# First linear of each GNN layer in groups of 512 nodes instead of 256, with the products chunk by chunk and the next group's turns between the chunks

## Chip, cores and metric

The kernel runs on one core of a Trainium2 chip. The metric is the device time of one execution in microseconds (us). One program computes a whole network; the change touches one of its stages, which runs four times.

## The reference, cut to what matters

The network works on 10000 nodes of 512 features. It has a relational graph layer, a mixture of experts, four graph layers of the kind below, and a quantized feed-forward part. The change touches `((1 + eps) * x + agg) @ W1 + b1` and what feeds its batch statistics:

```python
def _gine_layer(x, src, dst, edge_attr, eps, We, be, W1, b1, gamma, beta, W2, b2):
    e = edge_attr @ We + be
    m = jax.nn.relu(x[src] + e)
    agg = jax.ops.segment_sum(m, dst, num_segments=x.shape[0])
    h = ((1.0 + eps) * x + agg) @ W1 + b1        # the stage that changes
    mu = jnp.mean(h, axis=0)
    var = jnp.mean(jnp.square(h - mu), axis=0)
    h = (h - mu) * jax.lax.rsqrt(var + BN_EPS) * gamma + beta
    h = jax.nn.relu(h)
    return jax.nn.relu(h @ W2 + b2)
...
x = x + _L1_gnn_ref(_layernorm(x, axis=-1), ...)   # four such layers; the first reads layer-normed rows
```

## The kernel before, in words

Each of the four layers has three stages, kept apart by barriers on all engines: `message_phase` (gather, messages, sums per node), `hidden_phase` (the first linear, L2065 to L2215) and an output stage (the second linear). The layers are called first (layer 0), inner (layers 1 and 2, one loop body run twice) and final (layer 3); tiles carry these words in their names.

`hidden_phase` takes the nodes in `NG` = 40 groups: 39 of `GROUP` = 256 nodes and a last one of 16. A group goes through these steps, each on its own engine and each written as a loop over the groups by `static_pipeline`, which fixes the order of the work on every engine in advance:

- SP loads the 256 rows of x into `xin` (two buffers, which are halves of the weight buffer `raw`); a load waits until the turns of the group two before are done. The first 512 rows were loaded by the message stage. At the end SP fetches the next weight into `raw`.
- GpSimd gathers the aggregated sums, 128 rows at a time, into a ring of three buffers `agg` (L2109); gather j waits for mix j - 2. In layer 0 it also computes the row's reciprocal deviation `rs` (L183).
- In layer 0 alone (`normal`), VectorE takes the row statistics (L164, L168, L175), then `nb` (L2185), and ScalarE normalizes the rows in place (L2158).
- VectorE mixes: `(1 + eps) * x + agg` (L2196), one instruction for 128 rows.
- TensorE turns the mixed rows, eight 128x128 transposes a group into the PSUM tile `T` (L2132).
- ScalarE copies `T` to `xh` (L1177, the high part), VectorE subtracts to get `xl` (L1183, the low part), each one instruction over 4 chunks of 256 columns.
- TensorE forms the products (L783 to L785, called `three`): for each of 4 output chunks, for each of 4 input chunks, three matmuls with 256 moving columns: 48 a group. `xh`, `xl`, `T` and the result tile `O` have two buffers each; the two `T` take four PSUM banks and the two `O` the other four.
- ScalarE adds the bias and stores the four result chunks to `hT` (L2153), and VectorE takes batch statistics of pairs of groups (L2208).

TensorE's order is: turns of group g + 1, then products of group g. `keep_awake` (L791) runs matmuls on an identity at the start of a stage.

Of the kernel before, what the change touches and what calls it, by code (L numbers as in the profile page):

```python
# [10 lines left out]
P = 128  # L11
# [20 lines left out]
PAIRS = NG // 2 + 1  # L32
# [2032 lines left out]
def hidden_phase(core, cst, ed, table, eps, b1, w, layer, hT, stats, normal):  # L2065
# [5 lines left out]
    R, W = 3, 2  # L2071
    tiles = [(g, t, n) for g in range(NG) for t, n in tiles_of(g == NG - 1)]
    names = "eps eps1 b1 ld0 ld1 mix T hi lo M ev bn stats aggr var rstd nb nx w2 swg0 swg1 swg2"
    with core.phase("hidden", names) as (s, sbuf, psum):
        e_t = sbuf("eps", [P, 1])
        b1t = sbuf("b1", [P, KC])
        xin = [raw[:, q * TILES:(q + 1) * TILES, :] for q in range(2)]
        rbn, mv = ([sbuf(f"{n}{q}", [P, TILES, k]) for q in range(W)] for n, k in (("rbn", 6), ("mv", 2)))
        rs, nb = ([sbuf(f"{n}{q}", [P, TILES]) for q in range(W)] for n in ("rs", "nb"))
        agg = [sbuf(f"agg{i}", [P, D]) for i in range(R)]  # L2080
        xh = [sbuf(f"xh{q}", [P, KC, GROUP], F32R) for q in range(2)]
        xl = [sbuf(f"xl{q}", [P, KC, GROUP], F32R) for q in range(2)]
# [3 lines left out]
        last = lambda g: g == NG - 1  # L2086
        at = lambda g: slice(g * GROUP, g * GROUP + width_of(last(g)))
        mixed = lambda g: min((g + 1) * TILES, len(tiles))
        with nc.Block() as block:
            @block.sync  # L2090
            def _(eng):
# [7 lines left out]
                eng.wait_ge(s["T"], NG)  # L2099
# [4 lines left out]
            def _(eng):  # L2104
                def gather(j):
                    g, t, n = tiles[j]
                    c = g * TILES + t
# [3 lines left out]
                def rstd(g):  # L2111
                    wait(eng, s["nx"], g - W + 1)
                    row_rstd(eng, s, g, mv[g % W], cst.half, rs[g % W], last(g))

                if normal:
                    for j in range(R - TILES):
                        gather(j)
                    for g in range(NG):
                        for j in range(g * TILES + R - TILES, min(len(tiles), (g + 1) * TILES + R - TILES)):
                            gather(j)  # L2120
                        rstd(g)
                else:
                    static_pipeline([(0, gather)], len(tiles))
# [25 lines left out]
            def _(eng):  # L2149
# [12 lines left out]
                def high(g):  # L2162
                    split_hi(eng, s, g, g % 2, last(g), T, xh)
# [724 lines left out]
```

## Time and profile before

| | us |
|---|---|
| three runs | 4548.05, 4555.41, 4559.69 |
| median | 4555.41 |
| profiled execution, its own time | 4532.05 |
| its span in the trace | 4530.3 |
| mean granted clock of TensorE in the span | 0.913 |

Busy shares of the span: TensorE matmul 90%, its weight loads 74%, VectorE 61%, ScalarE 46%, GpSimd 34%. These are averages over stages with different limits. A matmul's duration in the trace is longer than its distance to the next one, since matmuls are pipelined: the distance from start to start is what a matmul costs in a dense row of them. The same holds, to a smaller degree, for dense rows of instructions on ScalarE and VectorE.

### The profile page before, as it was taken

The numbers are of one execution on the slowest core, as the hardware profiler recorded it, in microseconds if no ns is written. First come the engines' busy times: TensorE is split into PE (matmuls) and PEld (weight loads), VectorE is DVE, ScalarE is ACT, GpSimd is POOL, SyncE is SP. The second block draws the span as 40 slices with busy tenths as digits, with TensorE's granted clock in tenths as the row PEclk, the third lists the DMA queues.
The fourth block names the chain that finished last, engine by engine and source line by source line (L and its number), as shares of the span: only waits on it lengthen the run. The fifth ranks groups of instructions, "written<-read, shape, count | busy, mean of one in ns | idle before, by whom it ended". The sixth has DMA issues, their size and how long they took to land. (4 is left out here: it accounts for less than half of the span.)

```text
span 4530.3 us, 64838 instructions
## 1 busy us (share of the span) xinstructions
PE 4092.3 (90%) x22630; PEld 3331.6 (74%) x22630; DVE 2776.7 (61%) x5314; ACT 2065.9 (46%) x3536; POOL 1541.3 (34%) x1482
## 2 busy tenths in 40 slices
PE   7887899899978868789999999999899998999977
PEld 3446788777767656549988579987599784998855
DVE  5665656578975567557854455543555444556878
ACT  1222223333348334365567543475433674334556
POOL 1442266217840658744410233201332004330033
PEclk9998999999999568789999999999899998999965
DMA  8995478539975869874422565323754237554678
GB/s 302 400 336 179 151 261 283 183 123 348 390 273 163 296 143 174 156 234 153 155 89 106 172 205 165 107 94 136 237 162 140 77 119 242 159 161 126 185 194 248
DMA packets 460259, 886.19 MB, mean 196 GB/s; under 512 B 70660, under 2 KB 111221, under 8 KB 459182
## 3 DMA queue, kind: packets, MB, share of 16 engines
q1 hardware_dynamic: 291386, 520.05, 33.8%
q0 software_dynamic: 90016, 237.51, 18.9%
q10 hardware_dynamic: 78568, 124.88, 7.9%
q8 instruction: 168, 2.75, 0.2%
q14 instruction: 121, 0.99, 0.1%
HBM read 609.61 MB, written 303.62 MB: 202 GB/s over the span
## 5 line engine op out<-in xcount | busy, mean ns | idle before, releaser
L2109 POOL DMA_INDIRECT hidden_agg<-edge_sums,edge_where x316 | 354.6, 1122 | 711.3 <-DVE layer_raw_inner L2196 284.3
L1942 POOL DMA_INDIRECT message_x<-g,edge_partner x120 | 115.8, 965 | 755.6 <-POOLq L150 458.3
L783 PE MATMUL hidden_O<-hidden_xh,layer_hi_inner 128*128 128x256 f32 (+1 forms) x1280 | 366.9, 287 | 0.1
L785 PE MATMUL hidden_O<-hidden_xl,layer_hi_inner 128*128 128x256 f32 (+1 forms) x1280 | 361.0, 282 | 0.0
L784 PE MATMUL hidden_O<-hidden_xh,layer_lo_inner 128*128 128x256 f32 (+1 forms) x1280 | 360.2, 281 | 0.0
L2153 ACT ACTIVATE hT_inner<-hidden_O,hidden_b 128x256 f32<-128x256 f32 (+1 forms) x320 | 124.1, 471 | 332.6 <-PE hidden_O L785 332.6
L783 PE MATMUL root_O<-root_hi,root_xh 128*128 128x512 f32 (+1 forms) x632 | 255.4, 404 | 11.4 <-DVE root_xl L1183 10.2
L783 PE MATMUL output_O<-layer_hi_inner,output_hh 128*128 128x512 f32 (+1 forms) x632 | 250.2, 396 | 1.8 <-DVE output_hl L2290 1.8
L785 PE MATMUL output_O<-layer_lo_inner,output_hh 128*128 128x512 f32 (+1 forms) x632 | 249.7, 395 | 0.0
L784 PE MATMUL output_O<-layer_hi_inner,output_hl 128*128 128x512 f32 (+1 forms) x632 | 249.6, 395 | 0.0
L785 PE MATMUL root_O<-root_lo,root_xh 128*128 128x512 f32 (+1 forms) x632 | 247.9, 392 | 0.0
L2299 DVE TENSOR_TENSOR layer_raw_inner<-output_O,output_b2t 128x1024 f32<-128x1024 f32 x80 | 96.9, 1211 | 246.3 <-PE output_O L785 246.3
L784 PE MATMUL root_O<-root_hi,root_xl 128*128 128x512 f32 (+1 forms) x632 | 247.6, 392 | 0.0
L784 PEld LDWEIGHTS hidden_O<-hidden_xh,layer_lo_inner 128*128 128x128 f32 x1280 | 243.3, 190 | 0.0
L783 PEld LDWEIGHTS hidden_O<-hidden_xh,layer_hi_inner 128*128 128x128 f32 x1280 | 242.8, 190 | 0.6 <-DVE hidden_xl L1183 0.6
L785 PEld LDWEIGHTS hidden_O<-hidden_xl,layer_hi_inner 128*128 128x128 f32 x1280 | 243.0, 190 | 0.0
L1071 POOL DMA_INDIRECT root_agg<-edge_sums,edge_where x158 | 179.4, 1136 | 151.1 <-POOLq L150 68.7
L2208 DVE BATCH_NORM_STATS2 h_stats<-hT_inner 128x6 f32<-128x512 f32 (+2 forms) x168 | 97.6, 644 | 170.9 <-ACT hT_inner L2153 170.9
L1183 DVE TENSOR_TENSOR hidden_xl<-hidden_T,hidden_xh 128x1024 fp32r<-128x1024 f32 (+1 forms) x160 | 190.8, 1192 | 13.1 <-ACT hidden_xh L1177 13.1
L1078 POOL DMA_INDIRECT root_add<-edge_sums,edge_where_next x158 | 176.5, 1117 | 52.6 <-issue 47.3
L1177 ACT ACTIVATE hidden_xh<-hidden_T 128x1024 fp32r<-128x1024 f32 (+1 forms) x160 | 163.4, 1021 | 63.1 <-PE hidden_T L2132 61.4
L1177 ACT ACTIVATE root_xh<-root_T 128x1024 fp32r<-128x1024 f32 x80 | 80.5, 1008 | 243.9 <-PE root_O L785 87.9
(503 smaller groups left out, 12712.9 us busy)
## 6 DMA issues: line engine op xcount, KB each, us to landing
edge_sums<-message_res SPq DMA_DIRECT2D x160, 256.0 KB, 2.1
layer_raw_inner<-g SPq DMA_DIRECT2D x78, 512.0 KB
g<-layer_raw_inner SPq DMA_DIRECT2D x78, 512.0 KB
room<-in_L_gnn_basis SPq DMA_DIRECT2D x30, 1280.0 KB
order_basis<-in_L_gnn_basis SPq DMA_DIRECT2D x18, 1280.0 KB
edge_sums<-relation_res SPq DMA_DIRECT2D x82, 256.0 KB
order_x<-in_x SPq DMA_DIRECT2D x39, 512.0 KB
normed<-order_y ACTq DMA_DIRECT2D x39, 512.0 KB
```

The source lines that it names most:

```text
L783: eng.matmul(out, a_hi, b_hi, start=start, stop=False)
L784: eng.matmul(out, a_lo, b_hi, start=False, stop=False)
L785: return eng.matmul(out, a_hi, b_lo, start=False, stop=stop)
L1071: eng.indirect_dma_start(agg[q][0:n, t, :], None, ed.sums[0], bass.IndirectOffsetOnAxis(ap=ed.where[0][0:n, j:j + 1], axis=0)).then_inc(ga ...
L1078: eng.indirect_dma_start(add[q][0:n, t, :], None, ed.sums[0], bass.IndirectOffsetOnAxis(ap=ed.where_next[0:n, j:j + 1], axis=0), bounds_ch ...
L1177: eng.activation(xh[q][:, :, 0:w], T[q][:, :, 0:w], ACT.Copy).then_inc(s["hi"], 1)
L1183: eng.tensor_tensor(xl[q][:, :, 0:w], T[q][:, :, 0:w], xh[q][:, :, 0:w].bitcast(F32), ALU.subtract).then_inc(s["lo"], 1)
L1942: eng.indirect_dma_start(x[t % R][:, :], None, table, bass.IndirectOffsetOnAxis(ap=ed.partner[1][:, t:t + 1], axis=0)).then_inc(ga[t % R], 16)
L2109: eng.indirect_dma_start(agg[j % R][0:n, :], None, ed.sums[1], bass.IndirectOffsetOnAxis(ap=ed.where[1][0:n, c:c + 1], axis=0)).then_inc(g ...
L2153: m = eng.activation(hT[:, o, at(g)], O[g % 2][:, o, 0:width_of(last(g))], ACT.Identity, bias=b1t[:, o:o + 1])
L2208: eng.bn_stats(stats[:, o, g // 2 + last(g), :], hT[:, o, (g if g in alone else g - 1) * GROUP:at(g).stop]).then_inc(s["bn"], 1)
L2299: eng.tensor_tensor(part(y[q], last), part(O[q], last), b2t[0:n, :].unsqueeze(1).to_broadcast([n, k, D]), ALU.add).then_inc(s["add"], 1)
```

## The change

A group has `WIDE_GROUP` = 512 nodes (`PAIRS` = 20 groups: 19 of 512 and one of 272). `xin` becomes all of `raw` for even groups, and for odd groups the columns of `hT` that belong to the last but one group. Loads are of 512 rows. `T` is four whole PSUM banks, one for each input chunk, and `O` four, one for each output chunk; `xh` and `xl` have one buffer each, split by chunk. ScalarE's copy, VectorE's subtraction, and ScalarE's result step now work on one chunk of 512 columns each. TensorE does the products of input chunk c for all four output chunks (12 matmuls of 512 columns), then the four turns of chunk c of the next group, then chunk c + 1. The order on ScalarE and VectorE is written out by hand. The ring of gathers keeps its three buffers.

```diff
-    R, W = 3, 2
+    R = 3
+    PT = WIDE_GROUP // P
...
-        xin = [raw[:, q * TILES:(q + 1) * TILES, :] for q in range(2)]
+        xin = [raw.ap(), hT[:, :, at(PAIRS - 2)]]
-        xh = [sbuf(f"xh{q}", [P, KC, GROUP], F32R) for q in range(2)]
-        T = [psum(f"T{q}", [P, KC, GROUP]) for q in range(2)]
-        O = [psum(f"O{q}", [P, KC, GROUP]) for q in range(2)]
+        xh = sbuf("xh", [P, KC, WIDE_GROUP], F32R)
+        T = [psum(f"T{c}", [P, WIDE_GROUP]) for c in range(KC)]
+        O = [psum(f"O{o}", [P, WIDE_GROUP]) for o in range(KC)]
...
 SP
-                for g in range(2, NG):
-                    eng.wait_ge(s["T"], g - 1)
-                    eng.dma_start(part(xin[g % 2], last(g)), rows(table, g, last(g))).then_inc(ld[g % 2], 16)
+                for p in range(1, PAIRS):
+                    wait(eng, s["T"], (p - 1) * KC)
+                    f, begin = full(p), p * WIDE_GROUP
+                    eng.dma_start(xin[p % 2][:, 0:f, :], table[begin:begin + f * P, :]...).then_inc(ld[p % 2], 16)
...
 GpSimd
+                for j in range(R):
+                    gather(j)
+                for p in range(PAIRS):
+                    if normal:
+                        rstd(p)
+                    for j in range(p * PT + R, min(len(tiles), (p + 1) * PT + R)):
+                        gather(j)
...
 TensorE
-                static_pipeline([(0, turn_rows), (1, product)], NG)
+                turn_first()
+                for p in range(PAIRS):
+                    for c in range(KC):
+                        product(p, c)
+                        if p + 2 < PAIRS:
+                            turn_chunk(p + 1, c)
+                        elif p + 1 < PAIRS and c == 0:
+                            for each in range(KC):
+                                turn_chunk(p + 1, each)
...
 ScalarE
-                if normal:
-                    static_pipeline([(1, high), (0, norm), (2, evacuate)], NG)
+                for p in range(PAIRS):
+                    if p + 1 < PAIRS:
+                        high(p + 1, 0)
+                        high(p + 1, 1)
+                    if normal and p + 2 < PAIRS:
+                        norm(p + 2)
+                    if p + 1 < PAIRS:
+                        high(p + 1, 2)
+                    for o in range(KC):
+                        evacuate(p, o)
+                    if p + 1 < PAIRS:
+                        high(p + 1, 3)
...
 VectorE
-                if normal:
-                    static_pipeline([(4, statistics(0, KC - 1)), (1, shift), (2, low), (4, statistics(KC - 1, KC)), (1, mix), (0, row_statistics)], NG)
+                if normal:
+                    rows_ready(0)
+                for t in range(PT):
+                    mix(0, t)
+                for c in range(KC):
+                    low(0, c)
+                if normal:
+                    rows_ready(1)
+                for t in range(PT):
+                    mix(1, t)
+                for p in range(PAIRS):
+                    more, far = p + 1 < PAIRS, p + 2 < PAIRS
+                    if p >= 1:
+                        statistics(p - 1)
+                    if normal and far:
+                        row_statistics(p + 2)
+                    if more:
+                        low(p + 1, 0)
+                    if normal and far:
+                        shift(p + 2)
+                    if far:
+                        mix(p + 2, 0)
+                    if more:
+                        low(p + 1, 1)
+                    if far:
+                        mix(p + 2, 1)
+                    if more:
+                        low(p + 1, 2)
+                    if far:
+                        mix(p + 2, 2)
+                        mix(p + 2, 3)
+                    if more:
+                        low(p + 1, 3)
+                statistics(PAIRS - 1)
```

The waits that go with it: `turn_chunk(p, 0)` waits for all four mixes of group p; `product(p, c)` waits for `low(p, c)` and, at c = 0, for `evacuate(p - 1, o)` before output chunk o; `evacuate(p, o)` waits for the last matmul of output chunk o; `high` and `low` wait for the turns and the copy of their chunk. For the last group, `high` also waits until the products of the group before are nearly done, since `xh` has one buffer.

## Rows read from the trace of the kernel before

**Rows 1.** The page's first line.

```profile
span 4530.3 us, 64838 instructions
```

**Rows 2.** Windows by stage: hidden of layer 0, output of layer 0, hidden of layer 1; PE, PEld, DVE, ACT, POOL busy us (instructions), clock, DMA.

```profile
2050.00:2322.00 272.00, 269.53 (x2224) 265.59 (x2222) 207.80 (x418) 153.54 (x273) 108.18 (x111) 0.98 0.46 145
2330.00:2560.00 230.00, 225.09 (x966) 179.28 (x965) 96.07 (x85) 160.65 (x241) 2.14 (x3) 0.99 0.28 102
...
2657.00:2921.00 264.00, 262.66 (x2221) 262.33 (x2220) 143.38 (x199) 97.02 (x199) 82.50 (x73) 0.99 0.47 150
```

**Rows 3.** Timeline of TensorE, steady stretch of layer 1's hidden stage.

```profile
2800.81 1.04 PE L2132 MATMUL hidden_T<-cst_ident,layer_raw_inner 128*128 128x128 f32 x8
2801.61 0.36 PE L783 MATMUL hidden_O<-hidden_xh,layer_hi_inner 128*128 128x256 f32 x1
2801.81 0.28 PE L784 MATMUL hidden_O<-hidden_xh,layer_lo_inner 128*128 128x256 f32 x1
...
2899.31 1.04 PE L2132 MATMUL hidden_T<-cst_ident,layer_raw_inner 128*128 128x128 f32 x8
```

**Rows 4.** Timeline of TensorE: products 512 columns wide, in two other stages.

```profile
704.73 1.03 PE L1048 MATMUL root_T<-cst_ident,root_xin 128*128 128x128 f32 x8
...
705.84 0.39 PE L784 MATMUL root_O<-root_hi,root_xl 128*128 128x512 f32 x1
...
711.08 1.04 PE L1048 MATMUL root_T<-cst_ident,root_xin 128*128 128x128 f32 x8
...
2449.78 0.40 PE L785 MATMUL output_O<-layer_lo_first,output_hh 128*128 128x512 f32 x1
...
2455.85 0.40 PE L784 MATMUL output_O<-layer_hi_first,output_hl 128*128 128x512 f32 x1
```

**Rows 5.** Timeline of the 16-column group, layer 1, and a window over it.

```profile
2912.11 0.17 PE L783 MATMUL hidden_O<-hidden_xh,layer_hi_inner 128*128 128x16 f32 x1
...
2919.34 0.36 PE L785 MATMUL hidden_O<-hidden_xl,layer_hi_inner 128*128 128x16 f32 x1
...
2910.50:2920.00 9.50, 9.20 (x63) 9.10 (x62) 1.83 (x6) 0.74 0.05 20
```

**Rows 6.** Timelines of the beginnings: layer 1 (three rows), layer 0 (two rows).

```profile
2651.58 0.96 POOL L2109 DMA_INDIRECT hidden_agg<-edge_sums,edge_where  x1 [1.10 <-DVE layer_raw_inner L2196]
2655.17 0.75 DVE L2196 SCALAR_TENSOR_TENSOR layer_raw_inner<-layer_raw_inner,hidden_eps,hidden_agg 128x512 f32<-128x512 f32 x1 [0.96 <-DMA hidden_agg<-edge_sums,edge_where]
2657.11 0.39 PE L783 MATMUL hidden_O<-hidden_xh,layer_hi_inner 128*128 128x256 f32 x1
...
2036.79 1.29 DVE L164 BATCH_NORM_STATS2 hidden_rbn<-layer_raw_first 128x6 f32<-128x512 f32 x2
2050.40 0.56 PE L783 MATMUL hidden_O<-hidden_xh,layer_hi_first 128*128 128x256 f32 x1
```

**Rows 7.** Timelines and one group of lines: what ScalarE, VectorE and GpSimd instructions take.

```profile
2125.97 1.29 DVE L164 BATCH_NORM_STATS2 hidden_rbn<-layer_raw_first 128x6 f32<-128x512 f32 x2 [0.34 <-DMA layer_raw_first<-x]
2127.07 1.04 ACT L1177 ACTIVATE hidden_xh<-hidden_T 128x1024 fp32r<-128x1024 f32 x1
2127.95 0.72 POOL L183 TENSOR_TENSOR hidden_rs<-hidden_mv,cst_half 128x2 f32<-128x2 f32 x1
2128.86 1.22 DVE L1183 TENSOR_TENSOR hidden_xl<-hidden_T,hidden_xh 128x1024 fp32r<-128x1024 f32 x1
2128.98 1.52 ACT L2158 ACTIVATE layer_raw_first<-layer_raw_first,hidden_nb,hidden_rs 128x512 f32<-128x512 f32 x2 [0.87 <-DVE hidden_nb L2185]
...
2152.64 1.57 ACT L2153 ACTIVATE hT_first<-hidden_O,hidden_b 128x256 f32<-128x256 f32 x4 [1.47 <-PE hidden_O L785]
...
2789.49 2.47 DVE L2208 BATCH_NORM_STATS2 h_stats<-hT_inner 128x6 f32<-128x512 f32 x4 [4.17 <-ACT hT_inner L2153]
...
2924.94 1.41 POOL L2261 TENSOR_TENSOR output_rs<-output_mv,cst_half 128x4 f32<-128x4 f32 x1 [34.60 <-DVE output_mv L2269]
...
L2012 ACT ACTIVATE message_res<-message_B 128x512 f32<-128x512 f32 x5 | 2.8, 600 | 0.1
```

More of the change, by code:

```diff
@@ L2110, in gather, with rstd @@
                                            bass.IndirectOffsetOnAxis(ap=ed.where[1][0:n, c:c + 1], axis=0)).then_inc(ga[j % R], 16)
-                def rstd(g):
-                    wait(eng, s["nx"], g - W + 1)
-                    row_rstd(eng, s, g, mv[g % W], cst.half, rs[g % W], last(g))
-                if normal:
-                    for j in range(R - TILES):
-                        gather(j)
[L2118 to L2123, printed above, removed]
+                def rstd(p):
+                    wait(eng, s["nx"], through(p - 2) if p >= 2 else 0)
+                    eng.wait_ge(s["var"], p + 1)
+                    for n, ts in spans(p):
+                        m = eng.tensor_tensor(rs[p % 2][0:n, ts], mv[p % 2][0:n, ts, 1], cst.half[0:n, 0:ts.stop - ts.start], ALU.pow)
+                    m.then_inc(s["rstd"], 1)
@@ L2162, in high, with evacuate, norm @@
-                def high(g):
-                    split_hi(eng, s, g, g % 2, last(g), T, xh)
+                def evacuate(p, o):
+                    eng.wait_ge(s["M"], p * KC + o + 1)
+                    eng.activation(hT[:, o, at(p)], O[o][:, 0:width(p)], ACT.Identity, bias=b1t[:, o:o + 1]).then_inc(s["ev"], 1)
+                def norm(p):
+                    eng.wait_ge(s["nb"], p + 1)
+                    for t, n in tiles_of_pair(p):
+                        m = eng.activation(xin[p % 2][0:n, t, :], xin[p % 2][0:n, t, :], ACT.Identity,
+                                           bias=nb[p % 2][0:n, t:t + 1], scale=rs[p % 2][0:n, t:t + 1])
+                        m.then_inc(s["nx"], 1)
@@ L2164, in _, with high @@
+                def high(p, c):
+                    eng.wait_ge(s["T"], p * KC + c + 1)
+                    if p == PAIRS - 1:
+                        eng.wait_ge(s["M"], p * KC if c == KC - 1 else (p - 1) * KC + 1)
+                    eng.activation(xh[:, c, 0:width(p)], T[c][:, 0:width(p)], ACT.Copy).then_inc(s["hi"], 1)
                 eng.wait_ge(s["b1"], 16)
                 if normal:
-                    static_pipeline([(1, high), (0, norm), (2, evacuate)], NG)
-                else:
-                    static_pipeline([(0, high), (1, evacuate)], NG)
+                    norm(0)
@@ L2199, in statistics @@
-                def statistics(first, end):
-                    alone = range(NG - 2, NG)
-                    def step(g):
-                        if g % 2 == 0 and g not in alone:
-                            return
-                        eng.wait_ge(s["ev"], g + 1)
-                        for o in range(first, end):
-                            eng.bn_stats(stats[:, o, g // 2 + last(g), :], hT[:, o, (g if g in alone else g - 1) * GROUP:at(g).stop]).then_inc(s["bn"], 1)
-                    return step
@@ new lines, in statistics, with low, rows_ready @@
+                def statistics(p):
+                    for o in range(KC):
+                        eng.wait_ge(s["ev"], p * KC + o + 1)
+                        eng.bn_stats(stats[:, o, p, :], hT[:, o, at(p)]).then_inc(s["bn"], 1)
+                def low(p, c):
+                    eng.wait_ge(s["hi"], p * KC + c + 1)
+                    eng.tensor_tensor(xl[:, c, 0:width(p)], T[c][:, 0:width(p)], xh[:, c, 0:width(p)].bitcast(F32), ALU.subtract).then_inc(s["lo"], 1)
+                def rows_ready(p):
+                    row_statistics(p)
+                    shift(p)
```

138 lines of the change are left out of this document (78 added, 60 removed).

## Prediction

> **What bounds the kernel now.** I read the windows by stage first [rows 2]. The four hidden stages take 272 us in layer 0 and about 264 us in each of layers 1 to 3 (one of the three is shown; the others are alike), of a span of 4530.3 us [rows 1]. In all four TensorE is busy for 99% of the window at a granted clock of 0.98 or 0.99, so its own work sets the time. In layers 1 to 3 VectorE is busy 54% and ScalarE 37%, but in layer 0 VectorE is busy 207.8 of 272 us: the other engines have room in three layers and little in one. The timeline of TensorE then gives its prices, as distances from start to start.
>
> A steady group of 256 nodes takes (2899.31 - 2800.81) / 15 = 6.57 us [rows 3]: eight turns 0.80 us, one matmul 0.08 us late behind them, and 48 matmuls at 0.1185 us. Thus 512 nodes cost 13.13 us. The group of 16 nodes is nearly as dear as a full one: its 48 matmuls run from 2912.11 to 2919.34, 7.4 us, and the granted clock of that window falls to 0.74 on average, a mix of 2.4 and 1.2 GHz [rows 5].
>
> **TensorE's own work.** A matmul of 512 columns costs (711.08 - 705.84) / 23 = 0.228 us in the root stage, where 23 of them stand between those rows, and (2455.85 - 2449.78) / 26 = 0.2335 us in the output stage [rows 4]. I take 0.2305 between them, as nothing says which of the two this stage will resemble. One matmul of 512 then replaces two of 256 (0.237). The turns stay at 0.10 us each, but there are four switches in 512 nodes instead of two, each followed by a matmul that is 0.09 us late (704.73 to 705.84 is 1.11: 0.80 of turns, 0.23, and 0.09) [rows 4]. A group of 512: 48 x 0.2305 + 16 x 0.10 + 4 x 0.09 = 13.02 us, against 13.13: 0.1 us less, times 19 = 2 us a layer. With 0.228 and 0.2335 it is 4 us less or 1 us more. The width itself brings almost nothing, because a row of 256 is already paced near its columns.
>
> The last group: 256 columns at 0.1185 us and 16 more in proportion are about 0.126 us each, 6.05 us, where before there were 5.7 + 7.4 plus a small turn. This takes 7.3 us off each layer and is the one sure gain. At the end `high` of the last group waits for the group before, and the four result steps of 0.6 us come slower than the three matmuls of 0.38 us that wait for each: 1 us back.
>
> **The beginning of layers 1 to 3.** Before, the first product starts at 2657.11, 1.2 us after the fourth mix (2655.17 + 0.75) [rows 6], since the turns of group 1 come ahead of it. Now it also waits for four mixes, then a turn, a copy of 0.6 us (the 512-wide copy of L2012) [rows 7] and a subtraction of 0.67 us (half of 1.22 and a little): about 2657.8. Then comes a new wait. `turn_chunk(1, 0)` stands behind the first 12 matmuls (2.8 us, till 2660.5) and needs all four mixes of the second group. VectorE gets to them only after the four subtractions, at 2659.5. The gather of the fourth waits for the first of these mixes, since the ring has three buffers, and a gather takes 2655.17 - 2651.58 = 3.6 us to be usable [rows 6]. So 2660.2 + 0.3 + 3.6 = 2664.1, mix done at 2664.8. TensorE stands for 4.3 us, with product(0, 1) and everything else queued behind. Before, layer 0's first matmul took 0.56 us instead of 0.36 [rows 6, 3]: the lower level of the clock, 1.2 GHz. Its window lost 0.02 x 272 = 5.4 us to that level [rows 2], of which the last group's window has 0.26 x 9.5 = 2.5 [rows 5]; a cold start thus costs up to 3 us, and I add 2. Against the start of before this is 0.7 + 4.3 + 2 = 7 us.
>
> Sum for such a layer: -7.3 - 2 + 1 + 7 = about -1.5 to -2, say -2; three layers -6 us. Bounds: -8 (no low clock, 0.228) to +4 (0.2335, loads of 1 MB delaying the gathers at the start).
>
> **The steady state of layers 1 to 3.** VectorE has for 512 nodes four statistics (2.47 us for four), four subtractions (2.7) and four mixes (3.0): 8.2 of 13.0 us; ScalarE four copies (2.4) and four result steps (2.4). The load of 1 MB starts at T(p, 3) and has 6 us until the first mix wants it, 15 until TensorE does. These stay hidden; if the load took over 15 us it would not.
>
> **Layer 0.** Here the hand-written orders make a ring. `low(p, 3)` must be done before VectorE takes `statistics(p-1)` and `row_statistics(p+2)`; GpSimd's `rs` and VectorE's `nb` follow; `norm(p+2)` stands on ScalarE ahead of `high(p+1, 2)`, the four `evacuate(p, o)` and `high(p+1, 3)`; and `low(p+1, 3)` waits for that. Its length [rows 7]:
>
> - low: 0.06 + 0.67 us.
> - Batch statistics, four in a row: 2.4.
> - From the first row statistic to the first normalized row: before, 2128.98 - 2125.97 = 3.01 for two tiles. Two tiles more: 2 x 0.61 for the statistics, 0.17 for the aggregates, and `rs` on four columns takes 1.41 instead of 0.72: 5.1.
> - norm, four tiles: 1.52 + 2 x 0.71 = 2.9.
> - high: a copy of 512 takes 0.60, 0.53 in a row.
> - evacuate: 256 columns are 0.37 apart (1.57 for four); 256 columns more are (1.04 - 0.60) / 2 = 0.22: 4 x 0.59 = 2.4.
> - high again: 0.53.
>
> Together 14.6 us, against TensorE's 13.0: here the ring sets the time, and TensorE idles 1.6 us a group, in front of product(p+1, 0), which waits for evacuate(p, 0). Overlaps that I price too low or high give 13.8 to 15.2.
>
> ScalarE's result step is the row's extrapolation. The Trainium skill (ScalarE: Activation LUTs, section "What ACT_TABLE_LOAD costs") has 280 ns + 0.833 ns a column with a bias operand and 93 ns of overlap: 0.61 us at 512, an estimate, which would make the ring 0.1 us longer.
>
> The beginning: row statistics start at 2036.79 [rows 6], norm 5.1 later, first mix at 2042.7; the fourth waits for its gather until 2047.3 (2043.4 + 0.3 + 3.6); first product about 2049.7, against 2050.40. Then `rows_ready(1)` comes behind four subtractions (2051.5), its norm at 2056.6, mix(1, 0) done 2058.2, the gather for mix(1, 3) at 2062.1, done 2062.8. TensorE idles 10 us and starts again at the lower clock (2 us). Three more chunks of 3.26 us, and `high(1, 3)` ends at about 2076. Then 17 turns of the ring: 2076 + 17 x 14.6 = 2324.2. product(18, 0) starts 2.3 us before that; 12.4 for it, 0.7 and 6.05 for the last group: 2341. Before, the last product ends at about 2321.5. Layer 0 thus loses 20 us (6 at a ring of 13.8, 30 at 15.2).
>
> **Sum.** -6 + 20 = +14 us, on the profiled 4532 us: 4546. The three runs shown have the median 4555.4, 23 us above the profiled one, with no stage to put it to; I forecast against the median: 4569 us. Differences of 0.3% (13.7 us) are about what a measurement of this kernel tells from no change.
>
> **Rivals.**
>
> 1. *The ring does not bind (faster, or no change).* If its pieces overlap more and it falls to TensorE's 13.0 us, layer 0 gets 17 x 1.6 = 27 us back: -13, 4542. For it: TensorE was the limit in layer 0 too, at 207.8 us of VectorE work, and that work stays. Against it: the length is a sum of waits in a fixed order, not of busy time. The sign turns at a ring of 13.8 us. With the gathers at the start also in time (-4.3 -2 us in three layers) it is 4524. Chance 0.20.
> 2. *The gather of the fourth tile enters the ring.* gather(p+2, 3) waits for mix(p+2, 0) and has 4.5 us until `low(p+1, 3)` is due; it took 3.6 us with loads of 512 KB in flight. If the 1 MB load, which starts in the same microseconds, makes it 5 us or more, each group of layer 0 gains 0.7 to 1.5: +12 to +25 on the sum, 4581 to 4594. Chance 0.17.
> 3. *The clock falls at TensorE's idle of each group.* Before, layer 0 starts on the low level behind its long waits [rows 6], and the steady stretch has nearly none of it. If 1.6 us were enough, each group of layer 0 would lose up to 2 us of products, of which the idle absorbs most; +10 or so: 4580. Chance 0.08.
> 4. *Four banks in turn.* The output stage runs 512-wide products at clock 0.99 [rows 2], but twelve at a time into one bank; now the bank changes after every three. If the clock fell once in each wide group for the 2 us above, 57 groups in three layers would lose 114 us, and layer 0's 19, partly inside their idle, some 10: 4693. The Trainium skill (TensorE: Matmul & The Clock Gate, section "A second HAM failure mode: psum-queue depth-cycling") tells of 512-column products that cycle through banks, idle a little between groups and make the clock swing. No row of before cycles whole banks so. Chance 0.03.
>
> My forecast keeps 0.52. Its range is 4549 to 4587 (ring 13.8 to 15.2, the layers' bounds). The range that holds the time 8 times in 10 takes in rival 2 and the upper part of rival 1: 4532 to 4596. Faster by over 0.3%: the deeper half of rival 1 and a little of a common gain from 0.228, 0.18. Within 0.3%: a third of the forecast's case and the rest of rival 1, 0.39. Slower: 0.43.
>
> **What would show it.** In the changed profile: layers 1 to 3 hidden stages of 260 to 264 us from first to last product, TensorE idle once for about 4 us behind the first 12 matmuls, `hidden_T` waiting for the mix; matmuls of 512 at 0.23 us; no 16-column matmuls. In layer 0: about 290 us, TensorE waiting for `hT_first` (L783 behind the result step) 1 to 2 us a group, ScalarE's norm waiting for `nb`, and a distance of 14.6 us from group to group. The forecast is wrong if layer 0's groups are 13 us apart, or if those of the other layers are not.

## The result and the profile after

The changed kernel is slower by 0.8%: median 4585.89 us over 5 runs (4579.85 to 4587.9), against 4548.05 us over 5 runs (4538.01 to 4559.69) of the kernel before beside it. The ratio is 1.0077, 95% interval 1.0061 to 1.0094: +28 to +43 us against the kernel before beside it, where the forecast was +14. The page's first line of after, for the profiled execution ([rows 1] for before):

```profile
span 4584.1 us, 56575 instructions
```

Windows over the four hidden stages after, from first to last product (columns as in [rows 2]; layer 0, then layers 1 to 3):

```profile
2048.00:2361.00 313.00, 275.67 (x1258) 221.13 (x1259) 205.84 (x422) 141.17 (x231) 89.86 (x92) 0.92 0.38 123
2699.00:2962.00 263.00, 258.07 (x1256) 209.85 (x1257) 149.60 (x231) 96.24 (x157) 72.60 (x74) 0.98 0.47 148
3307.00:3568.00 261.00, 252.01 (x1248) 205.42 (x1248) 146.65 (x229) 95.70 (x156) 69.72 (x72) 0.99 0.47 146
3904.50:4165.00 260.50, 257.33 (x1260) 209.49 (x1260) 147.95 (x231) 95.91 (x157) 70.76 (x72) 0.98 0.47 148
```

Layer 0 took 272 us from first to last product at clock 0.98; now it takes 313 at 0.92, and TensorE is idle for 37 us of them. The other three are about as long as before. A fairer measure takes the start of a stage in: from the first `keep_awake` matmul of the hidden stage to the first one of the output stage. I use it below for every kernel.

| us per stage | layer 0 | layer 1 | layer 2 | layer 3 |
|---|---|---|---|---|
| before | 289.9 | 275.8 | 275.9 | 277.6 |
| after | 330.9 | 278.7 | 279.8 | 277.3 |

Layer 0: +41.0. Layers 1 to 3: +2.9, +3.9, -0.3. Their sum, 47.5 us, is nearly all of the 53.8 by which the profiled spans differ. The medians differ by 38; the profiled execution of before was faster than its median.

**The pace of layer 0.** Timeline of ScalarE, layer 0 after: the normalizations of three groups in a row (L2190; a group's four instructions are one row), and what stands behind the late one.

```profile
2196.50 2.94 ACT L2190 ACTIVATE layer_raw_first<-layer_raw_first,hidden_nb,hidden_rs 128x512 f32<-128x512 f32 x4 [2.27 <-DVE hidden_nb L2244]
...
2213.91 2.93 ACT L2190 ACTIVATE hT_first<-hT_first,hidden_nb,hidden_rs 128x512 f32<-128x512 f32 x4 [5.93 <-DVE hidden_nb L2244]
2216.75 0.58 ACT L2198 ACTIVATE hidden_xh<-hidden_T 128x512 fp32r<-128x512 f32 x1
2217.23 2.40 ACT L2185 ACTIVATE hT_first<-hidden_O,hidden_b 128x512 f32<-128x512 f32 x4
...
2228.11 2.94 ACT L2190 ACTIVATE layer_raw_first<-layer_raw_first,hidden_nb,hidden_rs 128x512 f32<-128x512 f32 x4
```

The distances are 17.4 and 14.2 us: the group in the buffer `hT` is late, the next one, in `raw`, less so. Over groups 2 to 18 the mean is 16.0 us, where I forecast 14.6. The timelines of SP, VectorE and TensorE show why the late one is late, and under them two rows of the waits of that stage (us in total, times, longest):

```profile
2200.10 0.36 SPq L2107 DMA_DIRECT2D hT_first<-x  x1
...
2209.32 2.47 DVE L2229 BATCH_NORM_STATS2 hidden_rbn<-hT_first 128x6 f32<-128x512 f32 x4 [3.51 <-DMA hT_first<-x]
...
2233.36 0.60 PE L2141 MATMUL hidden_T<-cst_ident,hT_first 128*128 128x128 f32 x4
2233.99 0.36 SPq L2107 DMA_DIRECT2D hT_first<-x  x1
```

```profile
PE hidden_O L784 <- DVE hidden_xl L2266: 30.2, 12, 4.2
DVE hidden_rbn L2229 <- DMA hT_first<-x: 23.1, 8, 4.0
```

The 1 MB load issued at 2200.10 released the row statistics at 2209.32, 9.2 us later. For layers 1 to 3 I had written that it "has 6 us until the first mix wants it". In layer 0 the first to want it is not the mix but VectorE's row statistics, which stand at the front of the ring. Statistics, norm and mixes of these rows follow, then their turns between the chunks of products, the last at 2233.36, and only then is the buffer free for its next load (2233.99): 33.9 us for two groups.

There is a second, smaller wait. Before every other group VectorE stands at the fourth mix of the group ahead until its gather has landed, though the copy that its next subtraction needs is done. The 1 MB load of the other buffer (issued at 2182.28 here) is in flight beside this gather, which makes it the likely cause. Timelines of ScalarE and VectorE:

```profile
2186.78 0.60 ACT L2198 ACTIVATE hidden_xh<-hidden_T 128x512 fp32r<-128x512 f32 x1
2188.28 0.75 DVE L2256 SCALAR_TENSOR_TENSOR hT_first<-hT_first,hidden_eps,hidden_agg 128x512 f32<-128x512 f32 x1 [2.29 <-DMA hidden_agg<-edge_sums,edge_where]
2188.95 0.69 DVE L2266 TENSOR_TENSOR hidden_xl<-hidden_T,hidden_xh 128x512 fp32r<-128x512 f32 x1
```

Eight subtractions are late by 0.5 to 2.7 us in this way, 10 us in the stage. Together with the 23.1 us of waits for loads this is nearly all by which 17 groups exceed the pace of 13.8 us that the kernel with three loads shows below.

TensorE's own timeline at that place, and windows of 4 us over it:

```profile
2213.23 0.60 PE L2141 MATMUL hidden_T<-cst_ident,layer_raw_first 128*128 128x128 f32 x4
2218.05 0.76 PE L784 MATMUL hidden_O<-hidden_xh,layer_hi_first 128*128 128x512 f32 x1 [4.21 <-DVE hidden_xl L2266]
2218.61 0.63 PE L785 MATMUL hidden_O<-hidden_xh,layer_lo_first 128*128 128x512 f32 x1
2219.03 0.63 PE L786 MATMUL hidden_O<-hidden_xl,layer_hi_first 128*128 128x512 f32 x1
```

```profile
2208.00:2212.00 4.00, 4.00 (x21) 3.27 (x20) 2.64 (x7) 0.00 (x0) 0.00 (x0) 1.00 0.07 26
2216.00:2220.00 4.00, 1.96 (x5) 1.60 (x6) 2.22 (x5) 4.00 (x8) 2.73 (x3) 0.65 0.86 323
2220.00:2224.00 4.00, 4.00 (x13) 3.12 (x12) 4.00 (x7) 0.11 (x1) 0.96 (x1) 0.50 0.50 156
2224.00:2228.00 4.00, 4.00 (x21) 3.31 (x20) 3.23 (x11) 1.08 (x2) 1.03 (x1) 1.00 0.01 3
```

TensorE stands for 4.21 us. The row names `hidden_xl`, but that had been done: product(p+1, 0) waits for evacuate(p, 0), which ScalarE starts at 2217.23 behind the late norm. After this idle time the matmuls are 0.42 us apart instead of 0.23: the granted clock is 0.50, the level of 1.2 GHz, from about 2217.2 until about 2224.0. Something like it happens at every other group between 2086 and 2316: eight idle stretches of 1.9 to 4.2 us, some 32 us apart, and at each of them a fall to 0.50 for some microseconds. At the other groups TensorE idles at most 0.8 us and the clock stays at 1.00.

**The beginning of layer 1 after**, timelines of VectorE and TensorE ([rows 6] for before):

```profile
2692.03 0.75 DVE L2256 SCALAR_TENSOR_TENSOR layer_raw_inner<-layer_raw_inner,hidden_eps,hidden_agg 128x512 f32<-128x512 f32 x1 [2.60 <-DMA hidden_agg<-edge_sums,edge_where]
2695.86 2.14 DVE L2256 SCALAR_TENSOR_TENSOR layer_raw_inner<-layer_raw_inner,hidden_eps,hidden_agg 128x512 f32<-128x512 f32 x3 [3.08 <-DMA hidden_agg<-edge_sums,edge_where]
...
2709.42 1.11 PE L2141 MATMUL hidden_T<-cst_ident,hT_inner 128*128 128x128 f32 x4 [4.08 <-DVE hT_inner L2256]
...
2715.03 0.63 PE L786 MATMUL hidden_O<-hidden_xl,layer_hi_inner 128*128 128x512 f32 x1
```

```profile
2702.00:2705.00 3.00, 3.00 (x8) 2.03 (x7) 0.25 (x1) 0.00 (x0) 0.94 (x1) 0.50 0.98 352
2705.50:2708.50 3.00, 0.00 (x0) 0.00 (x0) 1.11 (x2) 0.00 (x0) 0.95 (x1) 1.00 0.32 100
2709.00:2715.40 6.40, 5.98 (x16) 4.77 (x17) 1.72 (x3) 0.60 (x1) 3.08 (x3) 0.50 0.43 127
```

The stall of 4.08 us ahead of the turns of group 1 is where the prediction put it; in layers 2 and 3 it is 6.6 and 3.1 us. But the first product comes 13.3 us after the stage's first matmul (2686.58 to 2699.86), before 10.7 (2646.42 to 2657.11); in layers 2 and 3 it is 2.7 and 3.5 us later than before. In layer 1 the first 24 matmuls run at the low level, until about 2715.5. These are two falls and not one: the windows, whose third number from the end is the granted clock, show 0.50 in the first 12 matmuls, 1.00 during the stall, and 0.50 again behind it. In layer 2 the first 12 matmuls run at the high level and only those behind the stall at the low one.

In layer 0 the first product is 15.3 us behind the stage's first matmul (before 16.3), the stall ahead of group 1's turns is 7.3 us, and the granted clock is 0.50 for 15 of the first 19 us of products, before for the first 4.5.

### The profile page after: what moved, and what is told of

It reads as the page before. It is cut to its first block and busy times, and to the rows that moved or that the text cites. A ratio compares the mean times of both kernels' runs of the same rounds, so it can differ in the third digit from the quotient of the medians.

```text
span 4584.1 us, 56575 instructions
## 1 busy us (share of the span) xinstructions
PE 4078.2 (89%) x18790; PEld 3117.7 (68%) x18790; DVE 2789.4 (61%) x5420; ACT 2055.5 (45%) x3376; POOL 1488.7 (32%) x1463
## 5 line engine op out<-in xcount | busy, mean ns | idle before, releaser
L2198 ACT ACTIVATE hidden_xh<-hidden_T 128x512 fp32r<-128x512 f32 (+1 forms) x320 | 185.5, 587 | 655.4 <-PE hidden_T L2141 598.5
L2266 DVE TENSOR_TENSOR hidden_xl<-hidden_T,hidden_xh 128x512 fp32r<-128x512 f32 (+1 forms) x320 | 214.6, 676 | 175.9 <-ACT hidden_xh L2198 169.9
L784 PE MATMUL hidden_O<-hidden_xh,layer_hi_inner 128*128 128x512 f32 (+1 forms) x640 | 264.8, 414 | 2.2 <-DVE hidden_xl L2266 2.2
L786 PE MATMUL hidden_O<-hidden_xl,layer_hi_inner 128*128 128x512 f32 (+1 forms) x640 | 251.7, 393 | 0.0
L785 PE MATMUL hidden_O<-hidden_xh,layer_lo_inner 128*128 128x512 f32 (+1 forms) x640 | 250.5, 391 | 0.0
L657 PE MATMUL order_cb_ps<-room,order_spread 128*128 128x512 f32 x300 | 143.1, 623 | 28.7 <-DMA room<-in_L_gnn_basis 20.4
L784 PE MATMUL hidden_O<-hidden_xh,layer_hi_first 128*128 128x512 f32 (+1 forms) x320 | 139.0, 434 | 30.3 <-DVE hidden_xl L2266 30.2
L2406 ACT ACTIVATE hT_inner<-hT_inner,output_shf,output_scl (+2 forms) x312 | 159.6, 583 | 0.0
L1340 POOL TENSOR_TENSOR tokens_y<-tokens_y,tokens_rsd 128x1024 f32<-128x1024 f32 (+1 forms) x40 | 96.0, 2400 | 190.7 <-ACT tokens_y L1449 190.7
L1132 DVE TENSOR_TENSOR root_y<-root_O,root_agg 128x1024 f32<-128x1024 f32 x80 | 96.5, 1207 | 97.1 <-PE root_O L786 86.1
```

The lines of the kernel that those rows point to most:

```text
L657: m = eng.matmul(cb_ps[j % 2][:, :], spread[n][:, k, :], ba_t[i % RING][:, k % UNIT, :], start=k == 0, stop=k == SHARE - 1)
L784: eng.matmul(out, a_hi, b_hi, start=start, stop=False)
L785: eng.matmul(out, a_lo, b_hi, start=False, stop=False)
L786: return eng.matmul(out, a_hi, b_lo, start=False, stop=stop)
L2198: eng.activation(xh[:, c, 0:width(p)], T[c][:, 0:width(p)], ACT.Copy).then_inc(s["hi"], 1)
L2266: eng.tensor_tensor(xl[:, c, 0:width(p)], T[c][:, 0:width(p)], xh[:, c, 0:width(p)].bitcast(F32), ALU.subtract).then_inc(s["lo"], 1)
```

## Experiments

Ratios are to the kernel before, measured beside each on the same chip, with 95% intervals; the fourth column is the difference of the medians. Stage times are those of the one profiled execution. The chips differ: beside the last three kernels of the table the kernel before has a median of 4495.5 us, beside the others 4545 to 4548. The part of the profiled span outside the four stages, which no edit is meant to change, also differs from execution to execution: 3405 to 3447 us in the first nine kernels. So a stage's time is read for what an edit does in it, and the ratio for what it is worth.

| kernel | ratio | interval | us | layer 0 | layers 1, 2, 3 |
|---|---|---|---|---|---|
| changed | 1.0077 | 1.0061 to 1.0094 | +37.8 | 330.9 | 278.7, 279.8, 277.3 |
| layer 0 narrow | 1.0016 | 0.9996 to 1.0035 | +7.4 | 288.1 | 276.9, 278.2, 278.2 |
| layer 0 wide alone | 1.0094 | 1.0068 to 1.0119 | +39.9 | 316.0 | 275.3, 277.3, 277.4 |
| three loads | 1.0068 | 1.0043 to 1.0093 | +27.5 | 300.3 | 279.1, 279.7, 277.7 |
| statistics later | 1.0092 | 1.0069 to 1.0115 | +37.9 | 321.8 | 279.3, 278.3, 276.8 |
| both of these | 1.0002 | 0.9982 to 1.0023 | +5.0 | 284.6 | 279.1, 278.9, 277.4 |
| other beginning | 1.0015 | 0.9993 to 1.0038 | +10.4 | 329.3 | 268.0, 270.6, 267.7 |
| all three | 0.9956 | 0.9936 to 0.9976 | -18.6 | 280.7 | 271.6, 269.9, 269.0 |
| narrow, other beginning | 0.9951 | 0.9929 to 0.9974 | -23.6 | 288.5 | 267.6, 268.7, 268.2 |
| order alone | 1.0063 | 1.0039 to 1.0087 | +30.8 | 316.9 | 271.2, 271.6, 271.3 |
| load later alone | 1.0074 | 1.0044 to 1.0105 | +38.7 | 330.9 | 275.1, 275.8, 275.4 |
| three loads in layer 0 only | 0.9941 | 0.9921 to 0.9961 | -24.1 | 281.2 | 268.0, 268.6, 268.7 |

### Which layers

The narrow form of before (256 nodes, its batch statistics of the last two groups merged into one) in layer 0, and the reverse:

```diff
-                hidden_phase(core, cst, ed, table,
+                (narrow_hidden_phase if first else hidden_phase)(core, cst, ed, table,
```

> Layer 0's stage as before the change (groups of 256), layers 1 to 3 as after it. If the loss sits in layer 0, as the stage times say (+41 us there, about 0 in layers 1 to 3), this runs within 5 us of the kernel before, about 38 us under the changed kernel. If instead the wide form costs a little in every layer and layer 0's reading is an accident of one execution, it stays some 25 us or more over the kernel before.

> The reverse: the wide form in layer 0 alone, layers 1 to 3 as before the change. Loss in layer 0: about 38 us over the kernel before, within 5 us of the changed kernel. Loss spread over the layers: about 10 us over the kernel before.

+7.4 and +39.9 us: most of the loss is layer 0's. The first interval (-2 to +16 us) leaves room for the 1 to 3 us a layer that the stage times show for layers 1 to 3, and at its lower edge for no loss there at all.

The second kernel's trace also showed something new: its layer 0 has the same code as the changed kernel's and took 316.0 us, not 330.9. Its first half alternates like the one above; its second half does not. VectorE's timeline there:

```profile
2196.51 2.47 DVE L2229 BATCH_NORM_STATS2 hidden_rbn<-layer_raw_first 128x6 f32<-128x512 f32 x4 [0.50 <-DMA layer_raw_first<-x]
2210.32 2.46 DVE L2229 BATCH_NORM_STATS2 hidden_rbn<-hT_first 128x6 f32<-128x512 f32 x4
2224.91 2.48 DVE L2229 BATCH_NORM_STATS2 hidden_rbn<-layer_raw_first 128x6 f32<-128x512 f32 x4 [0.60 <-DMA layer_raw_first<-x]
```

Groups come evenly, 14.4 us apart (from 2186.63 to 2287.70 in seven), and a load issued at 2218.46 lands within 6.5 us. So the stage has two patterns, an even one near my 14.6 and an alternating one of 16, and slips from one to the other. Two kernels below give the same reading: "load later alone" has the changed kernel's layer 0 and took 330.9 us; "other beginning" and "order alone" have one and the same layer 0 and took 329.3 and 316.9. What makes it slip I did not find.

### The load or the ring

```diff
-        xin = [raw.ap(), hT[:, :, at(PAIRS - 2)]]
+        xin = [raw.ap(), hT[:, :, at(PAIRS - 2)], hT[:, :, at(PAIRS - 3)]]
-                    wait(eng, s["T"], (p - 1) * KC)
+                    wait(eng, s["T"], (p - 2) * KC)
```

> A third buffer for the table's rows, so that the 1 MB load of a group is issued one group (13 to 16 us) earlier. Theory A: in layer 0 every other group is held by a late load (row statistics wait 3.5 to 4.2 us on it, 23.1 us in 8 waits), and TensorE's idle behind it (about 4 us) is what lowers the clock; with the load early the waits on it fall to about 0, a group of layer 0 takes what the ring of VectorE, GpSimd and ScalarE takes, 14.2 to 14.8 us instead of a mean of 16.0, the granted clock stays at 1.0, and the time is 25 to 30 us under the changed kernel. Theory B: the four whole banks, or the clock by itself, make layer 0 slow: the group stays near 16 us and the time within 5 us of the changed kernel. Theory C: the ring alone makes 16 us and the wait on the load only takes up its slack: no wait on loads, still 15.5 to 16 us a group, less than 8 us gained.

The row statistics no longer wait for loads, the alternation is gone, and steady groups are 13.79 us apart (a few are longer, the mean over groups 2 to 18 is 14.05; timeline of ScalarE, then a window over eight groups):

```profile
2185.76 2.94 ACT L2190 ACTIVATE hT_first<-hT_first,hidden_nb,hidden_rs 128x512 f32<-128x512 f32 x4 [2.88 <-DVE hidden_nb L2244]
2199.54 2.94 ACT L2190 ACTIVATE hT_first<-hT_first,hidden_nb,hidden_rs 128x512 f32<-128x512 f32 x4 [2.30 <-DVE hidden_nb L2244]
2213.33 2.94 ACT L2190 ACTIVATE layer_raw_first<-layer_raw_first,hidden_nb,hidden_rs 128x512 f32<-128x512 f32 x4 [2.31 <-DVE hidden_nb L2244]
2227.12 2.94 ACT L2190 ACTIVATE hT_first<-hT_first,hidden_nb,hidden_rs 128x512 f32<-128x512 f32 x4 [2.31 <-DVE hidden_nb L2244]
```

```profile
2145.00:2255.00 110.00, 104.66 (x510) 84.09 (x509) 86.40 (x176) 58.27 (x96) 39.24 (x40) 1.00 0.46 153
```

TensorE still idles a little in each group (12.0 us in 16 waits, the longest 1.2), and behind those the clock stays at 1.00. Theory A's mechanism holds by the trace: no wait for a load, no fall of the clock, 30.6 us off layer 0's stage; its pace of 14.2 to 14.8 us a group was too long. By the medians only 10 to 12 us were gained instead of 25 to 30, and the interval overlaps that of the changed kernel. This kernel's six runs scatter from 4558 to 4592 us, and the profiled execution is the fastest of them; in time the gain of this edit by itself is not shown.

```diff
                 def statistics(p, first=0, end=KC):
...
-                    if p >= 1:
-                        statistics(p - 1)
                     if normal and far:
                         row_statistics(p + 2)
...
                         mix(p + 2, 1)
+                    if p >= 1:
+                        statistics(p - 1, 0, 2)
...
                         mix(p + 2, 2)
+                    if p >= 1:
+                        statistics(p - 1, 2, KC)
```

> VectorE's four statistics of the group behind are moved from ahead of the row statistics to behind the mixes 1 and 2 of the group ahead, in all layers; loads as after the change. If the ring (low of the last chunk, statistics, row statistics, GpSimd, shift, norm, high, evacuations) is what sets the groups whose load is in time, these get about 2 us shorter (from some 15 us to 13), and the groups with a late load stay near 17 or gain less, since the load is issued off TensorE's last turn and takes 8 us whatever VectorE does: 8 to 15 us under the changed kernel. If the load alone set the pace of both kinds of group, no change within 4 us.

No gain in the median, where 8 to 15 us were expected; the profiled layer 0 is 321.8 us, inside what the same form showed without this edit (316.0 and 330.9). Group by group the expectation is met in the middle of the stage: between groups 6 and 16 the late groups come 17.1 to 17.4 us behind the one before, the others 12.9 to 13.8. VectorE gets to its row statistics 2.4 us earlier and waits there: 39.6 us in 9 waits for the load, instead of 23.1 in 8. So with two buffers the load binds first and the ring behind it.

> The third buffer of the run with three loads and the statistics of the group behind moved back, together. With three loads a group of layer 0 took a regular 13.8 us, and nothing waited for a load. If that is the ring of VectorE, GpSimd and ScalarE, in which the four statistics take 2.4 us, moving them takes the ring under TensorE's own 13.0 us a group: layer 0's groups come at 13.0 us, the stage is some 15 us shorter than with three loads alone (285 instead of 300 us from its first TensorE instruction to the output stage's), and the time 12 to 18 us under that run, within 15 us of the kernel before. If 13.8 us is TensorE's own (turns, first products behind them), nothing changes against three loads alone, within 4 us.

The two together are worth more than their sum: the ratio falls to 1.0002, with an interval clear of the changed kernel's. ScalarE's timeline and a window of that kernel:

```profile
2195.96 2.92 ACT L2190 ACTIVATE hT_first<-hT_first,hidden_nb,hidden_rs 128x512 f32<-128x512 f32 x4
2208.92 2.93 ACT L2190 ACTIVATE layer_raw_first<-layer_raw_first,hidden_nb,hidden_rs 128x512 f32<-128x512 f32 x4
2221.88 2.92 ACT L2190 ACTIVATE hT_first<-hT_first,hidden_nb,hidden_rs 128x512 f32<-128x512 f32 x4
```

```profile
2145.00:2255.00 110.00, 110.00 (x545) 89.64 (x545) 91.03 (x187) 67.69 (x105) 42.18 (x43) 1.00 0.48 158
```

12.96 us a group, TensorE busy all the time, the stage 284.6 us (expected 285) and 15.7 shorter than with three loads alone. Behind the first groups the norm no longer waits for `nb`. That the ring of VectorE, GpSimd and ScalarE made 13.79 us is thereby shown: 2.4 us less in it, and TensorE sets the pace again.

### The beginning of a stage

```diff
+                for c in range(KC):
+                    product(0, c)
+                    for each in ((), (), (0, 1, 2), (3,))[c]:
+                        turn_chunk(1, each)
-                for p in range(PAIRS):
+                for p in range(1, PAIRS):
...
 SP, ahead of the load of group p
+                    if p == 1 and not normal:
+                        eng.wait_ge(s["mix"], 3)
```

> The changed kernel with another beginning of each stage only: TensorE does the products of chunks 0 to 2 of group 0 before the first turns of group 1, and in layers 1 to 3 the 1 MB load of group 1 waits for the third mix. Theory: the beginning of layers 1 to 3 costs about 10 us each (first product 2.6 us later because the load slows the gathers, 4.1 us stall ahead of the turns of group 1, half clock until some 13 us later). Then each of these stages gets 5 to 7 us shorter, layer 0 0 to 5 us (its pace is set by the loads), and the time is 15 to 25 us under the changed kernel. Rival: the wide groups of the steady state lose what is lost and the start does not matter: under 6 us gained.

Layers 1 to 3 are 10.7, 9.2 and 9.6 us shorter than after the change, more than expected; layer 0, paced by its loads, 1.6. The medians say 27 us less, where 15 to 25 were expected (the two kernels were measured on different chips, each beside the kernel before). The load now goes out at 2719.18, behind the gathers of group 0. TensorE's timeline of layer 1 in this kernel:

```profile
2722.62 0.50 PE L784 MATMUL hidden_O<-hidden_xh,layer_hi_inner 128*128 128x512 f32 x1 [1.15 <-DVE hidden_xl L2272]
2722.96 0.39 PE L785 MATMUL hidden_O<-hidden_xh,layer_lo_inner 128*128 128x512 f32 x1
...
2731.84 1.53 PE L2143 MATMUL hidden_T<-cst_ident,hT_inner 128*128 128x128 f32 x12 [0.56 <-DVE hT_inner L2262]
```

The first product is 11.3 us behind the stage's first matmul (2711.34), the stall is 0.56 us, and the products run at the high level from the start. Its two halves apart:

> Of the other beginning, the order of TensorE alone: products of chunks 0 to 2 of group 0 ahead of group 1's first turns; the load goes out at the stage's start as after the change. The other beginning as a whole made each of the stages of layers 1 to 3 9.9 us shorter. By the prediction's sum the stall at the turns (4.3 us) with its half clock (2) is most of it, the late first product 0.7 (2.6 as measured): this gains 6 to 7 us a layer, about 20 us in all against the changed kernel. If the load among the gathers is the larger part, under 3 us a layer.

> Of the other beginning, the load alone: in layers 1 to 3 the load of group 1 waits for the third mix, TensorE's order is that after the change. The first product comes 2 to 3 us earlier, but group 1's first turns still wait for the fourth mix of group 1, whose gather waits for its first mix: 2 to 4 us a layer, 6 to 12 us in all against the changed kernel; if the two parts of the other beginning do not add, 7 us a layer or more.

By the stages (means of layers 1 to 3) the order alone gives 7.2 us a layer, the later load alone 3.2, both together 9.8: they nearly add, as the sum of stall, clock and late product would. The medians do not resolve this: +30.8 and +38.7 us against the kernel before, with intervals of some 22 to 27 us' width. The order was expected to come 20 us under the changed kernel, and by the ratios it is about 6; the later load 6 to 12 us, and it is about 1. So the split is read from the stages alone, one execution each. In the kernel with the later load alone the first product is 11.5 us behind the first matmul, but a stall of 3.5 us in layer 1 and the low clock behind it stay; in that with the order alone the stall is gone and the first product is as late as after the change (13.6).

### Together

> Three loads, statistics moved back, and the other beginning, together. If the three causes (late load and ring in layer 0, beginnings of all layers) are all of the loss, it is the sum of the others: layer 0's stage 280 to 285 us, layers 1 to 3 271 to 273 us each, and the time 10 to 25 us under the kernel before. If the parts do not add (the loads that start earlier slow the gathers), it is at the kernel before or above.

> Layer 0 as before the change, layers 1 to 3 wide with the other beginning. With the wide layers at 13.0 us a group against 13.1, the end 7 us shorter and the start down from 10 to some 4 us: 3 to 5 us gained a layer, 8 to 15 us under the kernel before. If the wide form has no gain outside the start, within 5 us of the kernel before.

> Everything that helped where it helped: three loads in layer 0 only (in layers 1 to 3 two, since there the third made a stage 1 to 4 us longer), statistics moved back, the other beginning in all layers. Layer 0's stage 281 us, layers 1 to 3 268 us each: 5 to 8 us under the run with everything in all layers, 20 to 30 us under the kernel before.

In the first and third of these the load of group 2, where there is a third buffer, also waits for group 0's mixes; no run has this wait by itself. All three beat the kernel before, by 0.4 to 0.6%. With everything in all layers it is -18.6 us, the stages as expected or up to 2 us better; with layer 0 left narrow and the wide form with its other beginning in layers 1 to 3 -23.6 us, more than the 8 to 15 expected. The lowest ratio, 0.9941 or -24.1 us, is that of the kernel with the third buffer in layer 0 only, as expected; the three intervals overlap. Windows of its layers 0 and 2:

```profile
2035.00:2300.00 265.00, 257.43 (x1260) 209.42 (x1258) 202.37 (x423) 146.56 (x232) 89.72 (x92) 0.98 0.45 145
...
3209.00:3459.00 250.00, 250.00 (x1248) 204.20 (x1246) 146.05 (x227) 94.88 (x155) 67.18 (x72) 1.00 0.47 152
```

In two of the layers 1 to 3 the third buffer had made a stage 1 to 4 us longer; without it there they take 268.4 us on average. This kernel and the one with layer 0 narrow differ by less than their intervals, so whether layer 0 is better wide or narrow is open by time, and 7 us in favour of wide by its one profiled stage.

## Why the prediction was right, and where it was off

The direction is right, and so are layer 0 as the place of the loss and a ring as its kind. That the time of 4586 us lies in the forecast range, at its upper edge (4587), is in part luck. The range stood on the earlier median of the kernel before, 4555; against that median it allows a loss of up to 32 us, and the loss was 38. The largest part of the loss, the wait for the load in layer 0, was no term of the sum, while a ring priced 0.8 us too long stood in for a third of it: with the ring of 13.8 us that the runs show, the prediction's own sum comes to 0. Rival 2's range (4581 to 4594) also holds the time; its mechanism is in the trace, but not as the main one.

- **TensorE's own work: right.** Forecast 13.02 us a group. Measured 12.96 in layers 1 to 3 (a load, issued off TensorE's last turn, at 3925.11, 3938.07 and 3951.02) and in layer 0 once nothing else bound it. Clock 0.98 to 0.99 in layers 1 to 3, the rest of it at the beginnings: the banks in turn (rival 4) did nothing. The page of the Trainium skill that rival 4 named (TensorE: Matmul & The Clock Gate, section "A second HAM failure mode: psum-queue depth-cycling") describes a clock that swings in 512-column bf16 products that cycle through banks, where TensorE also idles a little between the groups. Here the cycling without idle time left it at 1.00 for 250 us, and so did cycling with idle time of 0.6 to 1.2 us once a group (three loads). The falls in the steady part of layer 0 stand at idle stretches of 1.9 us and more; how much of them is the cycling's, no run separates.
- **Last group, -7.3: right, 0.1 to 0.7 too much.** The products of the last group run in 6.3 us from first to last start (2956.10 to 2962.40 in layer 1), where the last two groups took 13.0, 12.9 and 13.5 us in layers 1 to 3 (in layer 1 from 2906.32 to 2919.34, [rows 5]): -6.6 to -7.2. The "1 us back" behind it does not appear: 2.5 to 2.9 us from the last product to the output stage, before 2.8. With the start mended, a wide stage takes 268.4 us against 276.4: -8.0.

```profile
2956.10 0.29 PE L784 MATMUL hidden_O<-hidden_xh,layer_hi_inner 128*128 128x272 f32 x1
...
2962.40 0.28 PE L786 MATMUL hidden_O<-hidden_xl,layer_hi_inner 128*128 128x272 f32 x1
```

- **Beginning of layers 1 to 3, +7: right in kind, too small.** The stall was forecast at 4.3 us and is 4.08 in layer 1 (6.6 and 3.1 in layers 2 and 3). The late first product was forecast at 0.7 and is 2.6; 2.0 of this goes away when the load of 1 MB is not issued among the gathers (11.3 instead of 13.3 us), and the prediction had the load there only as a bound. The low clock was put at 2 us and in layer 1 covers 24 matmuls at 0.43 instead of 0.23 us apart, 4.8. That is 11.5 instead of 7, and would turn -2 a layer into +2.5; the stages show +2.2 as a mean. (-7.3 - 2 + 1 + 7 is -1.3 and not -2, too, and the range by its own bounds 4553 to 4589.)
- **Layer 0, the ring: right mechanism; its terms 0.8 us too long.** By the rows of the kernel with three loads it is 13.79: low 0.61, statistics 2.37, row statistics to norm 4.58, norm 2.84, high 0.48, evacuate 2.27, high to low 0.64. Forecast 14.6. The largest miss is the third term (5.1), as `rs` on four columns takes 1.04 us here, not the 1.41 taken from another stage [rows 7]. The result steps, the row's extrapolation, are 2.27 for four where 2.4 stood.
- **Layer 0, +20 in all: the step that failed.** "The load of 1 MB starts at T(p, 3) and has 6 us until the first mix wants it" was said of layers 1 to 3. Even there VectorE's mixes wait for it, mostly up to 4.8 us and once, in layer 2, 6.7, but TensorE saw it only that once, for 2.2 us at 3446.77. For layer 0 no such margin was worked out, although row statistics want the load a whole norm earlier than the mix, at the front of the ring. The late loads take 6.2 to 9.2 us, and that is a second, longer ring: load, statistics, norm, mixes, the four turns between the chunks, next load of the same buffer. The beginning was right in sum: `high(1, 3)` ends 42.0 us behind the stage's first matmul, forecast 41.9. From there to the end of `high(18, 3)` the 17 groups take 268.6 us, 15.8 each, where 17 x 14.6 is 248.2: 20.4 us, where 21 are missing.
- **Rival 3 was half true:** the clock does fall at idle time, but at the 1.9 to 4.2 us of every other group; with up to 1.5 us in each group (even half of "layer 0 wide alone") it stayed at 1.00. **Rival 2** (the fourth gather) was half true as well: beside the load the fourth gather comes late before every other group, by 0.5 to 2.7 us, and 13.8 us plus this delay is the distance of these groups within 0.1 us (14.2 at 0.46, 15.3 at 1.56). What the 10 us cost is open, since without them the group behind might only wait longer for its load; the third buffer took away the waits for loads and most of this, and no experiment sets them apart. **Rival 1** is what the repaired kernel shows, 12.96, and not the changed one.
- The two misses have one sign, about 4 us in each of three layers and 21 in layer 0, 33 us by the stages. By the medians the change costs 38 us where 14 were forecast, 24 more. The time itself, 4586 against 4569, came nearer, since the forecast stood on a median of the kernel before that was 7 us higher than the one measured beside it.

## What to carry to other kernels

When two buffers are made twice as long, check for every consumer, in each variant of the stage, who is first to want the load, and how long the load takes at its new size beside the other traffic: a ring through a DMA does not show in busy times. When an order of work is written out by hand, add up the ring of waits across engines; here, moving 2.4 us of work that nobody waits for out of it gave back the pace, but only after the load was early too. And a steady state that works says nothing of the first group: products that are ready should stand ahead of turns that must wait.

## What the runs showed of the hardware

- Around the end of an idle stretch of 4.2 us on TensorE the granted clock was 0.50 for 6.8 us, 6.0 of them under the matmuls that followed; in the same stage it also fell at idle stretches of 1.9, 3.0, 3.1 and 3.2 us. Waits of up to 1.2 us in each group (kernel with three loads) left it at 1.00. With 12 matmuls 0.19 us slower, that stall of 4.2 us cost 6.5.
- Loads of 1 MB took from 6.2 to 9.2 us to release a waiting reader in layer 0 of the changed kernel, with gathers in flight, and once 11.3 us in layer 2 (issued at 3428.82, mix at 3440.11). Issued at the start of layer 1's stage, such a load made the first gather usable after 4.9 us instead of 3.5, and the second after 7.4 instead of 3.8 (from the issue to the mix that takes it).
- The same code of layer 0 took 316.0 us in one kernel and 330.9 in two, with even and alternating groups; another form of it took 316.9 and 329.3. A loop that is bound by a ring through a DMA can have two patterns, and one trace does not show it.
